# Cross attention and top-2 experts on one core: twelve expert tiles listed in attention, the last two batches routed inside the expert stage

## What is computed

```python
h = layernorm(x)
q, k, v = heads(h @ Wq.T + bq), heads(ctx @ Wk.T + bk), heads(ctx @ Wv.T + bv)      # 16 heads of 32
x = x + (softmax(q @ k.T / sqrt(32)) @ v) @ Wo.T + bo
flat = layernorm(x)                                                                # 4096 tokens
scores = softmax(flat @ router_weight.T + router_bias)                             # 8 experts
w = the 2 highest scores of each token, 0 elsewhere
gu = flat @ gate_up_proj[e] + gate_up_bias[e]                                      # 512 -> 2 x 512
gate, up = min(gu[:512], 7), clip(gu[512:], -7, 7)
act = (up + 1) * gate * sigmoid(1.702 * gate)
out = x + sum over e of w[e] * (act @ down_proj[e] + down_bias[e])
```

## Time and profile before

| | us |
|---|---|
| median of 3 runs | 1718.96 (1716.83 to 1722.5) |
| the profiled execution | 1718.58 |
| its span | 1716.9 |
| TensorE busy in the span | 1589.1 (93%) |
| VectorE busy | 1273.5 (74%) |
| ScalarE, GpSimd busy | 656.7, 836.2 |
| mean granted TensorE clock | 0.976 |

### The profile page before, as it was taken

One profiled execution on the slowest core, in us unless ns is written; L12 is line 12 of the kernel. 1 busy time (PEld: TensorE's weight loads), 2 busy tenths in 40 slices (PEclk: granted clock), 3 DMA queues, 4 the chain that ended last, 5 costly groups with the idle time before them and its releaser, 6 DMA issues. The chain is left out here.

```text
span 1716.9 us, 30244 instructions
## 1 busy us (share of the span) xinstructions
PE 1589.1 (93%) x9612; PEld 1164.3 (68%) x9612; DVE 1273.5 (74%) x2414; ACT 656.7 (38%) x1267; POOL 836.2 (49%) x634
## 2 busy tenths in 40 slices
PE   6799999999999999999998469999999999999995
PEld 4455555555555555555553169999999998999994
DVE  5575777878668778787685668778888778777873
ACT  3354544535445445454444133223333233223320
POOL 3365656466566666666777322333333333333332
PEclk9899999999999999999999869999999999999998
DMA  6342433343434434424331161324543253324321
GB/s 221 80 124 71 108 113 86 112 106 87 124 80 113 102 91 101 121 73 114 98 89 32 60 222 55 101 82 168 173 146 128 89 209 117 115 84 148 113 87 61
DMA packets 101125, 188.99 MB, mean 110 GB/s; under 512 B 28192, under 2 KB 29600, under 8 KB 100960
## 3 DMA queue, kind: packets, MB, share of 16 engines
q1 hardware_dynamic: 79936, 124.25, 25.6%
q0 software_dynamic: 20832, 62.49, 11.4%
q10 hardware_dynamic: 192, 0.26, 0.0%
HBM read 204.32 MB, written 37.51 MB: 141 GB/s over the span
## 5 line engine op out<-in xcount | busy, mean ns | idle before, releaser
L802 DVE TENSOR_REDUCE negmax<-max_ps 128x2 f32<-128x1024 f32 x252 | 307.2, 1219 | 163.3 <-PE max_ps L542 163.1
L671 ACT ACTIVATE pt<-work 128x512 f32<-128x512 f32 x512 | 278.4, 595 | 290.4 <-PE work L554 281.1
L983 POOL TENSOR_TENSOR acc<-acc,pt 128x1024 f32<-128x1024 f32 x128 | 303.8, 2376 | 129.7 <-ACT pt L671 129.7
L1486 PE MATMUL gu_ps<-xgT_hi,wg_hi 128*128 128x256 f32 x1248 | 349.6, 280 | 1.5 <-DVE xgT_lo L1601 1.5
L1486 PE MATMUL gu_ps<-xgT_lo,wg_hi 128*128 128x256 f32 x1248 | 346.2, 277 | 0.0
L1486 PE MATMUL gu_ps<-xgT_hi,wg_lo 128*128 128x256 f32 x1248 | 346.1, 277 | 0.0
L980 POOL TENSOR_TENSOR acc<-pt 128x1024 f32<-128x1024 f32 x64 | 153.3, 2396 | 195.4 <-PE work L574 126.5
L1486 PEld LDWEIGHTS gu_ps<-xgT_hi,wg_hi 128*128 128x128 f32 x1248 | 235.5, 189 | 2.0 <-issue 1.9
L1486 PEld LDWEIGHTS gu_ps<-xgT_lo,wg_hi 128*128 128x128 f32 x1248 | 235.8, 189 | 0.1
L1486 PEld LDWEIGHTS gu_ps<-xgT_hi,wg_lo 128*128 128x128 f32 x1248 | 235.5, 189 | 0.0
L1747 POOL DMA_INDIRECT out<-acc,token_of x78 | 77.1, 989 | 323.2 <-DVE acc L1645 317.4
(11 more groups left out here) (221 smaller groups left out, 2894.9 us busy)
## 6 DMA issues: line engine op xcount, KB each, us to landing
raw_g<-w_gate_up SPq DMA_DIRECT2D x39, 2048.0 KB
raw_d<-w_down SPq DMA_DIRECT2D x39, 1024.0 KB
qs<-q_hi SPq DMA_DIRECT2D x252, 64.0 KB
ks<-k_hi SPq DMA_DIRECT2D x252, 64.0 KB
bd<-b_down SPq DMA_DIRECT2D x39, 256.0 KB
x_in<-x SPq DMA_DIRECT2D x36, 256.0 KB, 3.4
ctxT_raw<-ctx_t SPq DMA_DIRECT2D x32, 256.0 KB, 4.0
xln_dram<-x SPq DMA_DIRECT2D x32, 256.0 KB, 2.3
```

What stands on the lines that cost most here:

```text
L671: e.activation(pt[k % 2][:, h, :], in_work("exp", u, k, h)[:, :], ACT.Exp, scale=scale).then_inc(exped.sem, 1)
L802: e.tensor_reduce(negmax[:, u % 2, n:n + 2], pair_of(u, r)[:, :, :], AX.X, ALU.max, negate=True).then_inc(maxed.sem, 1)
L983: e.tensor_tensor(acc[:, heads, :], acc[:, heads, :], pt[k % 2][:, heads, :], ALU.add).then_inc(added.sem, 1)
L1486: ins = e.matmul(gu_ps[n % GU_BANKS][:, part, :], wg[s][pw][:, k, cols], xgT[s][px][:, k, :], start=(k == 0 and m == 0), stop=(k == KD - 1 ...
```

## The change

The last group of token tiles is now the last two batches (8 tiles), and attention routes the six groups before it. The list of tiles has two parts. The first 12 (`EARLY`) are whole tiles of the first five batches' tokens: their counts are taken in the units 27 and 28 (`whole_count` on TensorE, `whole_tiles` and `whole_rows` on VectorE), SP fetches their token numbers from `token_list` with twelve small copies of 128x2 numbers (`whole_tokens`), each after a register load, and then loads the weights of the first two tiles (`load_early`); VectorE and ScalarE split the first set while attention ends, and GpSimd gathers the rows of tiles 0 and 1 (`fetch_early`). The other 27 tiles are found out in the expert stage: the routing of the last group is cut into generators whose pieces VectorE does behind the quarters of the tiles, two a quarter in tile 0 and one a quarter from tile 1 on (`route`); TensorE does its matmuls in the middle of gate_up of the tiles 1, 7, 8 and 9 (`EARLY_STEPS`), into the bank of the transposes; GpSimd lists 2 token tiles an iteration in four iterations. `routing_stage` and its barrier are gone. `wd_lo` is written over `raw_d`, so a down load waits for the down matmuls of two tiles before. ScalarE's `down_hi` stands behind the first quarters' sigmoids instead of ahead of them. Since the main list starts all experts anew, weights are loaded at 14 tiles: 0, 1, 5, 7, 8, 12, 13, 17, 18, 24, 25, 30, 34 and 38.

```diff
+EARLY = 12
+EARLY_STEPS = (1, 7, 8, 9)
+LIST_SPREAD = 4
-    return [(n, batch) for n in range(0, last, batch)] + [(last, batch - 1), (last + batch - 1, batch + 1)]
+    return [(n, batch) for n in range(0, last, batch)] + [(last, 2 * batch)]
...
+            if s == EARLY_END + 7:
+                at(2, ("whole_count",))
+                at(3, ("whole_tiles",))
+            if s == EARLY_END + 8:
+                at(3, ("whole_rows",))
+            if s == units[-1]:
+                at(2, ("whole_tokens",), *[("load_early", part) for part in "gd"])
+            if s == units[-1] + 1:
+                at(0, ("load_early", "g1"))
+                at(1, ("token_of",), *[("split_early", k) for k in range(C)])
+                at(2, ("fetch_early", 0), ("fetch_early", 1))
...
-            g = groups[-2]
-            if s == units[-1] + 1:
-                at(1, ("best", g, 0), ("best", g, 1), ("count", g), ("rank", g))
-                at(2, ("place", g), ("soft", g))
-            if s == units[-1] + 2:
-                at(0, *[("list", g, t) for t in range(GROUPS[g][1])])
-                at(1, ("share", g))
-                at(5, *[(kind, g + 1, *what) for kind, *what in (("best", 0), ("best", 1), ("count",), ("soft",), ("rank",), ("place",))])
...
+            def early_lo(k):
+                e.wait_ge(early["wg_hi_made"][0], k + 1)
+                e.tensor_tensor(early["wg0"][1][:, k, :], early["raw_g"][0][:, k, :], early["wg0"][0][:, k, :].bitcast(F32),
+                                ALU.subtract).then_inc(early["wg_lo_made"][0], 1)
...
+                elif kind == "whole_tokens":
+                    e.wait_ge(rows_made, 1)
+                    e.wait_ge(early["listed"], 16 * TOP_K * EARLY_END)
+                    for i in range(K):
+                        row = e.value_load(early["row"][0:1, i:i + 1], min_val=0, max_val=E * NT - FTOK // P)
+                        e.dma_start(token_in[:, i, :], token_list[bass.ds(row, FTOK // P), :].rearrange("r q -> q r"),
+                                    allow_slow_non_contiguous=True).then_inc(tokens_in, 16)
...
-def routing_stage(nc, route, stored, w_rows, w_stored, token_list, listed, tile_hot, tile_expert, tile_changed, token_of, n_tiles, groups, first_loads):
...
+                    for at_tile, what in zip(EARLY_STEPS, HANDED):
+                        if half == 0 and i == at_tile + 2:
+                            e.wait_ge(taken.sem, taken[what])
...
-                    gate_up(i + 1, range(KF))
+                    gate_up(i + 1, range(KF // 2))
+                    if i + 1 in (RANK_AT, LIST_AT, FIRST_AT, RUN_AT):
+                        e.wait_ge(xgT_lo_made.sem, xgT_lo_made[i + 2, 0])
+                    if i + 1 == RANK_AT:
+                        rank_last()
...
+                    gate_up(i + 1, range(KF // 2, KF))
...
-                    down_hi(i + 1, changed_flag(e, i + 1))
...
+                    if f == 1 and now:
+                        down_hi(now, changed_flag(e, now))
...
+            chain = {(0, 0): (best_experts(0), best_experts(1), count_experts()), (RANK_AT, 2): (share(), place_tokens(), main_tiles()),
+                     (LIST_AT, 2): (take_list(),), (FIRST_AT, 2): (take_first(),), (RUN_AT, 2): (take_run(),)}
...
+                    route(now, f)
+                    if now < RANK_AT:
+                        route(now, None)
...
+            def load_down(i):
+                s = i % 2
+                if i >= 2:
+                    e.wait_ge(down_made.sem, down_made[i - 2, SUB - 1])
```

817 lines of the change are left out of this document (511 added, 306 removed).

## The result

The change makes the kernel slower: 1737.36 us median of four runs (1732.56 to 1741.89) against 1720.73 for the kernel before (1716.83 to 1722.73), ratio 1.0105 with a 95% interval of 1.0085 to 1.0125. The forecast was 1711 us, within 1697 to 1727, with 0.13 for slower. The profiled execution of after has a span of 1730.8 us, 13.9 more than that of before.

A forecast was written before the change was run, and what follows sets the result against it. TensorE, busy for 93% of the span, was taken as the bound, so only its holes could be gained. −31.4 at the seam, +32.4 expert-stage stalls, −8.6 for before's stalls: −7.6 from 1718.58 gives 1711 us, range 1697 to 1727.

The forecast's parts named there:

- The gain at the seam: Between attention and expert stage: first gate_up matmul at 978.2 instead of 1009.60, 31.4 us earlier.
- reciprocals: End of attention: VectorE's reciprocals, on which TensorE's last projections hang, start 3.5 us later, bounds −1 and +8.
- The release stays late: Rival, attention's end: GpSimd's DRAIN or the jump out of attention costs the 8 us again; 1719 us, chance 0.13.
- SP's copies are slow: Rival, attention's end: twelve list copies at 2.9 us each delay the early weight loads; 1726 us, chance 0.13.
- Tile 1: Middle of tile 1's gate_up: TensorE waits 9.5 us for xgT_lo, plus 2.4 for the clock, 11.9 in all.
- The pairs of reloads: Tiles (12, 13), (17, 18), (24, 25), weights loaded twice in a row: stalls of 2.95 us each, 8.8 in all.
- The sign given for them: Trace sign for the reload pairs: three TensorE waits for acc of 2 to 3 us near tiles 12, 17 and 24.
- Tiles 7 to 9: Reload pair at 7 and 8 with late routing pieces: stalls of 6.3 us, bounds 2.4 to 8.3.
- Tile 5: One reload at tile 5 with late routing pieces on VectorE: a stall of 2.6 us, bounds 0 to 4.6.
- A plain tile takes 17.26: Expert stage: a tile without new weights takes 17.26 us, taken over from the kernel before.
- The tail's 1.8: End of the kernel: one reload in the very last tile costs 1.8 us, bounds 0 to 2.6.
- larger stalls: Rival, expert stage: every reload pair costs its old 4.16 us, tiles 5 and 7 to 9 their upper ends; 1719, chance 0.11.

The follow-up runs named there:

- a_fitnolist: The kernel after with operands back at the kernel before's distances and the sixteen late list scatters left out; ratio 1.0005 to before.
- a_nolist: The kernel after without the sixteen late list scatters, the last two batches' rows missing from the list; ratio 1.0031 to before.
- a_fit: The kernel after with unused bytes putting xgT and hid at the distance from their weights that the kernel before had; ratio 1.0086 to before.
- a_half: The kernel after with eight of the sixteen late list scatters left out; a single execution, 1746.33 us.
- b_x64: The kernel before with 64 unused bytes ahead of xgT and all that lies behind it; ratio 1.0101 to before.
- b_w64: The kernel before with 64 unused bytes ahead of the split weights and 64 more ahead of xgT; ratio 1.0072 to before.
- b_probe: The kernel before with xgT of even tiles at 288 and odd tiles at 448 modulo 512, weights at 32; ratio 1.0051 to before.
- a_relist: Kernel after, operands at before's distances, six list scatters issued again at attention's end, each pair waiting for the one before; ratio 1.0244 to before.

## Why the prediction was wrong

Two steps failed. The sum had no term for what GpSimd issues for the late routing: the sixteen list scatters and the longer last drain cost 12.7 us. And it took a plain tile at 17.26 us after as before, where it takes 17.67 to 17.78; that cost 4.5 us on top. The other 8.5 of the 26 us between forecast and measurement are spread over terms that it did have.

**The gain at the seam was right**, −31.1 for −31.4, and by its own steps: SP's copies 1.4 (1.55), reciprocals 2.6 later (3.5), the release at 974.5 (974.7), gate_up 3.4 after TensorE's first transposes (3.47). That it met to 0.3 us is luck, as the eight executions lie between −25.9 and −32.6. "The release stays late" fell: the release is 0.2 us after the last engine's drain and TensorE's transposes begin 0.1 us after it, so the 8.1 us that the rule of the Trainium skill ("Runtime: NRT & Kernel Launch", section "Instruction fetch mechanics") would have brought back did not come; whether this jump left the fetched window no view shows. "SP's copies are slow" fell too, at 1.4 apart. The 2.0 us of the Trainium skill ("DMA: Bandwidth & Descriptors", section "Anatomy of one DMA — SWDGE (gpsimd) path") stand there for GpSimd's path and are mostly the time until completion is known; these copies were SP's, and they did not pay it one after the other. (The 1724 given for it was added up wrongly; by the rival's own working 2.6 us each make 1722.9.) One more step hit by luck: the drain of GpSimd was to end before 968, ended at 974.3, and happened to meet VectorE's.

**Tile 1 was right**: 11.7 for 11.9, of it 8.4 of wait for 9.5.

**The pairs of reloads were right at the pace for which they were worked out**: 2.95 each, measured 2.3, 3.0 and 2.9 in a_fitnolist. In after they are 1.1 to 1.3 each, as a slower TensorE leaves VectorE more room. The sign given for them, three waits for `acc` of 2 to 3 us, was too large: they are 1.4 to 1.6 us in a_fitnolist, with up to 0.5 more a tile earlier.

**Tiles 7 to 9 were put too low**: 6.3 was forecast and 8.3 the bound, 9.9 measured in a_fitnolist (four periods from rows 7). The term counted no fall of the clock, and TensorE's granted clock is 0.93 there in the second period (0.86 in a_nolist). Tile 5 was put too high, 2.6 for a measured 1.4.

**"A plain tile takes 17.26" is the step that failed without being seen as one.** I took the matmuls' time as given by their shapes and the clock. In after 36 periods carry 0.46 us more each, 17 us, by where the buffers lie. It would be wrong to call that its price, since a_fit gave back only 0.2% (some 3 us, within the noise), a_fitnolist against a_nolist 0.26% (4.5 us, hardly outside it): in this kernel what the pace costs is largely what VectorE's lateness would cost otherwise. In the sum: rows 12 to rows 38 were +9.7 where +3.8 was forecast: 12 more by the pace, and 6.2 less because stalls forecast at 9.8 were 3.6.

**The list scatters stood in no term.** The prediction has VectorE's part of the late routing, piece by piece, and nothing of what GpSimd issues for it, though GpSimd's queue is also that of the gathers and of the output's reads and writes. They cost 6.8 us between rows 2 and rows 12 (205.8 against 199.0 in a_nolist) and 5.9 in the last drain.

**The tail's 1.8 became 6.2**: 5.3 more between the last issue and the end, as GpSimd's drain is 5.9 us longer and begins 0.6 sooner after that issue; 1.6 more up to TensorE's last gap, where the waits add up to the same as in before and the rest is pace; 0.7 less from there to the last issue. The single reload in the tail, the only term that I had, is worth 1.5 us.

By the ratios, the scatters with their drain are 12.7 us of after's 18, the pace 4.5 on top of that, and 0.9 remain, where my own terms said −7.6. a_fitnolist shows where these 8.5 us are, as far as one execution can: 3.9 at the seam (q to G0 is 65.3 instead of 61.4), 2.6 in the tail, 1.9 from rows 2 to rows 12 (tiles 7 to 9, less what tiles 1 and 5 stay under their forecast), 0.8 ahead of q, 0.3 from rows 12 to rows 38, and 1.1 less from G0 to rows 2. At the seam the clock differs. From 968 to 975 its granted clock is 0.50, the 1.2 GHz level, and after's 0.98 (window, length, busy time and count by engine, clock, DMA share, GB/s; first after, then a_fitnolist):

```profile
968.00:975.00 7.00, 3.92 (x43) 2.90 (x44) 1.44 (x6) 2.32 (x7) 1.24 (x4) 0.98 0.54 203
```

```profile
968.00:975.00 7.00, 5.76 (x37) 4.12 (x35) 2.29 (x7) 2.13 (x5) 1.30 (x3) 0.50 0.82 313
```

In the stretch before, 960 to 968, TensorE was busy for 5.1 us at 0.93 in after and for 5.9 at 0.71 here. Why the clock fell in one and not in the other no run here shows.

**The chances.** No rival had a mechanism off VectorE, SP and the barrier; "larger stalls" (1719) was the nearest in kind and still 18 us short; "SP's copies are slow" (1726) was nearer in number, by a mechanism that did not occur. The range's upper end was built from known terms at their bounds and held no room for a resource that no term named.

## What to carry to other kernels

When an edit moves buffers, the pace of matmuls far from the edit can change: look first at the time of one unchanged, gap-free group in the new trace, and if it differs, put the moving operand and the weights back at their old distance. Price what an edit queues on each engine, and on GpSimd's above all, where small scatters hold up large gathers behind them and lengthen the next drain, even one that is 600 us away. And where VectorE has as little room as here (12.6 of 17.3 us in a plain tile, 17.6 of 21.0 at a pair of reloads), a gain on TensorE can be eaten by waits for VectorE, so cost an edit against both. Last, profile more than one execution before trusting a piece of the span: the same seam took from 60.1 to 66.9 us.

## What the runs showed of the hardware that I had not expected

- 96 matmuls of 128x256 (fp32r) take 10.98 us or up to 11.60 at the same granted clock 1.00, by where their two operands lie: 64 unused bytes cost 5.6%. The table above has eight distances and no more; I have no rule that explains all of them. The same distance at other places gave the same pace (448 in before and a_fit, 0 in b_x64 and b_w64).
- GpSimd's drain at the end of the kernel takes 2.01 us if only scatters and gathers of rows were issued in the expert stage (before, a_nolist), and 7.894 if eight or sixteen scatters of 4-byte entries were among them (a_half, after), the last one some 600 us before. At the end of attention, which issues many, it is 5.6 to 6.1, and where such scatters are the last thing issued it ends 8.7 to 9.7 us behind the last of them (before, b_x64, b_w64, b_probe, a_relist). What it does in that time no view shows.
- A pair of scatters of 4-byte entries has landed 7.4 to 8.4 us after the second's issue (a_relist), and with four of them an iteration GpSimd's wait for a write of rows is 5.4 to 9.9 us instead of 2.0 (after).
